# A seven-tile ring for gathered rows, norms made ahead, and the end of an attention laid among mixture blocks

## The chip, the core and the metric

The kernel runs on one core of a Trainium2 chip, as one launch. The core has five engines that work in parallel, each strictly through its own list of instructions: TensorE (PE, matmuls, with the loading of weights shown as PEld), VectorE (DVE), ScalarE (ACT), GpSimd (POOL) and SyncE (SP). They meet only at semaphores. SP and ACT issue plain transfers, POOL issues the indirect ones (a gather or scatter of 128 rows of 128 numbers by a list of row numbers). The metric is the time on the device in microseconds (us), the median of the runs.

## The reference

Two layers over x, 64 sequences of 64 tokens of 128 numbers (4,096 tokens, 32 tiles of 128), in float32:

```
x = x + tanh(g_xattn[0]) * attention0(layernorm(x), ctx, ctx)   # rope, band of 32, 16 heads of 8
x = x + tanh(g_ffn[0])   * mixture0(layernorm(x))               # 64 experts of 88, 8 per token, 1 shared
x = x + tanh(g_xattn[1]) * attention1(layernorm(x), ctx, ctx)   # full in a sequence, biases
x = x + tanh(g_ffn[1])   * mixture1(layernorm(x))               # 8 experts of 512, 2 per token
```

A mixture routes each token to its experts, weighs their results and adds them: `rw` holds 8 (then 2) weights per token, `out[t] = sum_e rw[t,e] * mlp_e(x[t])`.

## The kernel before, in words

Four stages follow each other on PE. **Attention** (L = 0, then 1) is a pipeline over 16 groups of 256 tokens (2 tiles). Step j does six things at once: the front of group j (f), the scores of group j-1 (m), the values of j-2 (v), the output, residual and second norm's statistics of j-3 (b), the router of j-4 (r), and the rank of each row within its expert of j-5 (k). There are 21 steps, so the last five only drain the pipeline.

**The first mixture** (`experts`) takes rows that POOL has scattered by expert into `expert_rows`: 16 shared batches, then 96 routed batches of 4 blocks of 128 rows, 48 for each half of the tokens. Batch by batch, PE turns and multiplies (L729, L747, L762, L775), ACT takes the silu (L985) and copies the result out (L993), DVE multiplies and copies (L1449, L1457), ACT's queue stores 256 KB to `expert_results`. **The combination**: POOL gathers each tile's 8 result rows per token (`gather`, L1634, 8 gathers a tile, 256 in all) and DVE adds them into x with 8 dependent instructions (`combine`, L1539). Tiles 0 to 15 (first half) go into a ring of four tiles in `xn2T`, tiles 16 to 31 into a ring of four in `late_rows`; POOL waits until the tile four before has been combined (`s_comb`). Tiles 0 to 9 are combined during the first mixture, one every four batches and all 8 instructions in a row; the other 22 during attention 1, where `combined_at` names the step.

**Attention 1's first norm** needs x with all 8 results added. DVE takes the statistics of group j at the head of step j (`norm_stats`, L1101, L1105), POOL makes 1/deviation of them (`deviation`, L1660, L1662), DVE the shift `nm` (L1118), ACT applies it (`xn`, L884). POOL's list for step j is: deviation of group j, 6 gathers, the second norm's deviation of group j-3 (same lines), 6 gathers; when the gathers are out, scatters for the second mixture (`scatter_late`, L1641) stand in their place. Before step 0 stand the gathers of tiles 0 to 13.

**The second mixture** (`late_experts`) is 80 blocks of 128 rows: DVE copies weights (L1554), PE multiplies up (L813) and down (L823), ACT takes the gelu (L1022). It begins when attention 1 has drained on every engine. After it POOL gathers the last 32 pieces (L1655), DVE adds them, SP stores x.

**The start**: SP issues the constants, two tables of 576 and 65 KB, 8 tiles of x, nine small inputs behind one count (`S["weights"]`), then the other 24 tiles. PE, ACT (tanh of the gates) and DVE (`split_row`, the bias row in three bf16 parts) all wait for the whole count.

The order is written out by hand: each engine's list is the program text, and no planner moves anything.

## Time and profile before

| | us |
|---|---|
| median of 3 runs (1228.23 to 1237.3) | 1228.86 |
| the profiled execution | 1228.1 |
| its span, first to last instruction | 1226.3 |
| mean granted PE clock, share of full | 0.875 |

The profiled execution is 1.8 us longer than its span and 0.8 us under the median. By the trace, attention 0 runs from the start to about 290 us, the first mixture to 667.1, attention 1 to 1019.8, the second mixture to 1175 and the last gathers, sums and stores to 1226.3. To read it: times of the trace count from the span's start; "idle before <- X" is the time that an engine stood still and the instruction that released it; a transfer is named by its target and source (`expert_results<-arena` is the first mixture's store). Where a step or a batch is spoken of, its start is found in the trace by the instruction that occurs once in each.

### The profile page before, as it was taken

Reading aid. Unit: us, or ns where it says so; the run is one execution under the profiler, and the core shown is the slowest. Engines: PE = TensorE matmul, PEld = TensorE weight load, DVE = VectorE, ACT = ScalarE, POOL = GpSimd, SP = SyncE. Lnnn points to the kernel's source line nnn. Section 1 sums busy time; section 2 is a strip of 40 time slices with the busy share of each in tenths; the row PEclk is TensorE's granted clock in tenths of the full one; section 3 lists DMA queues with packets and bytes.
Section 4 is the critical chain, followed back from the end, with each engine's and each line's share of the span. In section 5 each row is a group of like instructions: output and inputs, shape, how many; then the busy total and the mean of one; then the engine's idle time right before and its main releaser. Section 6 shows DMA issues by size and latency. Waiting matters only on the chain.

```text
span 1226.3 us, 27918 instructions
## 1 busy us (share of the span) xinstructions
PE 968.1 (79%) x8822; PEld 830.1 (68%) x8822; DVE 741.0 (60%) x2638; ACT 600.2 (49%) x1497; POOL 675.9 (55%) x749
## 2 busy tenths in 40 slices
PE   2888889855899999999896357977678778999930
PEld 1666666643699989988896136765556557999930
DVE  3678888866677778655555336567666554334422
ACT  1566666622245545545553143645445535666610
POOL 1106777777777750277555556767767643005445
PEclk9999999966999999999998556668778878999965
DMA  6434666523547765677665222332222112223322
GB/s 184 109 87 118 181 195 175 149 66 103 155 148 216 219 197 161 183 206 207 195 196 161 75 63 75 84 95 77 53 56 83 40 53 69 79 78 109 100 71 66
DMA packets 251184, 151.47 MB, mean 124 GB/s; under 512 B 56179, under 2 KB 236579, under 8 KB 251043
## 3 DMA queue, kind: packets, MB, share of 16 engines
q1 hardware_dynamic: 164706, 68.91, 20.5%
q0 software_dynamic: 20480, 41.98, 11.7%
q10 hardware_dynamic: 65856, 38.81, 10.8%
q8 instruction: 76, 1.25, 0.4%
q14 instruction: 66, 0.53, 0.2%
HBM read 77.24 MB, written 72.35 MB: 122 GB/s over the span
## 4 chain that ended last, share of the span: by engine, by line
PE 51%; DVE 17%; POOL 11%; issue 7%; ACT 6%; DMA 6%; SPq 1%; POOLq 0%; DVEq 0%; ACTq 0%
PE bank L747 6%; PE bank L813 6%; PE bank L823 6%; DVE x L1539 6%; PE bank L775 5%; DMA expert_results<-arena 5%; PE bank L557 4%; PE bank L570 3%; PE bank L762 3%; POOL expert_rows L1619 2%; POOL late_rows L1655 2%; PE bank L729 2%; PE bank L586 2%; PE bank L535 2%; POOL expert_rows L1641 2%
## 5 line engine op out<-in xcount | busy, mean ns | idle before, releaser
L1619 POOL DMA_INDIRECT expert_rows<-xn2T,slot x256 | 250.8, 980 | 88.6 <-issue 82.9
L1634 POOL DMA_INDIRECT xn2T<-expert_results,slot x128 | 122.5, 957 | 131.6 <-DMA expert_results<-arena 61.0
L1634 POOL DMA_INDIRECT late_rows<-expert_results,slot x128 | 123.9, 968 | 48.0 <-issue 36.3
L557 PE MATMUL bank<-cst,work 128*128 128x128 f32 x512 | 96.3, 318 | 51.4 <-ACT sg L943 43.1
L747 PE MATMUL bank<-wexp,arena 128*128 x768 | 135.1, 319 | 0.0
L1655 POOL DMA_INDIRECT late_rows<-expert_results,slot1y x64 | 62.2, 972 | 128.4 <-DMA expert_results<-yb 99.4
L890 ACT ACTIVATE work<-bank 128x512 f32<-128x512 f32 x128 | 76.6, 598 | 96.2 <-PE bank L557 94.4
L775 PE MATMUL bank<-wexp,arena 88*128 x768 | 106.3, 281 | 17.1 <-DVE arena L1457 13.3
L747 PEld LDWEIGHTS bank<-wexp,arena 128*128 128x128 f32 x768 | 114.6, 190 | 5.1 <-issue 1.2
L1022 ACT ACTIVATE arena<-bank,wcopy 128x128 f32<-128x128 f32 x320 | 91.3, 368 | 51.8 <-PE bank L813 51.8
L985 ACT ACTIVATE arena<-bank 128x176 f32<-128x176 f32 x224 | 69.3, 317 | 92.8 <-PE bank L747 52.2
L1457 DVE COPY arena<-bank 88x512 f32<-88x512 f32 x112 | 76.5, 683 | 61.4 <-PE bank L762 57.7
L775 PEld LDWEIGHTS bank<-wexp,arena 88*128 88x128 f32 x768 | 93.1, 191 | 27.4 <-issue 25.4
L557 PEld LDWEIGHTS bank<-cst,work 128*128 128x128 f32 x512 | 64.1, 158 | 61.1 <-issue 57.8
L570 PEld LDWEIGHTS bank<-vm,work 128*64 128x64 f32 x2048 | 81.2, 156 | 32.1 <-ACT work L890 21.3
L993 ACT ACTIVATE arena<-bank 128x512 f32<-128x512 f32 x96 | 57.3, 597 | 87.8 <-DMA expert_results<-arena 50.2
L1449 DVE TENSOR_TENSOR arena<-arena,bank 128x176 f32<-128x176 f32 x224 | 70.7, 333 | 47.2 <-ACT arena L985 45.5
L570 PE MATMUL bank<-vm,work 128*64 128x18 f32 x2048 | 94.3, 227 | 5.0 <-ACT work L890 4.6
L1123 DVE TENSOR_REDUCE nmax<-bank 128x8 fp32r<-128x512 f32 x128 | 85.1, 672 | 9.9 <-PE bank L541 8.5
L884 ACT ACTIVATE xn<-x,nm,rs 128x128 f32<-128x128 f32 x64 | 28.0, 487 | 126.3 <-DVE nm L1118 118.7
L813 PE MATMUL bank<-xgT,wcopy 128*128 128x128 f32 x640 | 86.1, 279 | 1.1 <-DVE wcopy L1554 1.1
L586 PE MATMUL bank<-arena,wqk 128*128 128x256 f32 x192 | 63.6, 445 | 26.6 <-DVE arena L1138 11.4
(207 smaller groups left out, 2118.3 us busy)
## 6 DMA issues: line engine op xcount, KB each, us to landing
arena<-expert_rows SPq DMA_DIRECT2D x384, 64.0 KB
expert_results<-arena ACTq DMA_DIRECT2D x96, 256.0 KB
expert_rows<-zero SPq DMA_DIRECT2D x288, 64.0 KB
arena<-in_ctxT ACTq DMA_DIRECT2D x32, 256.0 KB
expert_rows<-xn2T,slot POOLq DMA_INDIRECT x320
xg<-expert_rows SPq DMA_DIRECT2D x80, 64.0 KB
expert_results<-yb ACTq DMA_DIRECT2D x20, 256.0 KB
wx<-in_mix SPq DMA_DIRECT2D x16, 256.0 KB
```

Source lines behind the costliest of these rows:

```text
L557: mm = pe.transpose(w[:, bb * P:(bb + 1) * P], work[:, u, bb * P:(bb + 1) * P], ident)
L570: mm = pe.matmul(w2[b2 * SEQ:(b2 + 1) * SEQ, at:at + 2 * VW], work2[:, u % 2, pair * P + b2 * SEQ:pair * P + (b2 + 1) * SEQ], vm[:, V % 3, ...
L586: mm = pe.matmul(w[:, h * GTOK:(h + 1) * GTOK], wqk[:, n, h * P:(h + 1) * P], rhs, start=True, stop=True)
L747: mm = pe.matmul(out[:, b * 2 * I0:(b + 1) * 2 * I0], xgT[:, n % 2, 2 * h + b, :], wflat[:, bass.ds(offsets[m][2 * h + b], 2 * I0)], start ...
L775: mm = pe.matmul(bank[7][:, b * P:(b + 1) * P], hT[0:I0, n % 2, b, :], wflat[0:I0, bass.ds(offsets[m][b] + 2 * I0, P)], start=True, stop=T ...
L813: mm = pe.matmul(bank[2 + i % 3][:, c * P:(c + 1) * P], wcopy[:, i % WRING, c * P:(c + 1) * P], xgT1[:, m % 2, i % NB, :], start=True, sto ...
L890: act.activation(work2[:, u % 2, :], (w0, w3, w3, w3)[u][:, :], ACT.Copy).then_inc(S["pt_copied"], 1)
L1022: a = act.activation(hT1[:, i % WRING, c, :], bank[2 + i % 3][:, c * P:(c + 1) * P], ACT.Gelu_apprx_tanh, bias=wcopy[:, i % WRING, F1 + c: ...
L1123: dve.tensor_reduce(nmax[:, u, :], score[u][:].rearrange("p (a k) -> p a k", k=SEQ), AX.X, ALU.max, negate=True).then_inc(S["max_done"], 1)
L1619: pool.indirect_dma_start(xs, bass.IndirectOffsetOnAxis(ap=slot[:, t, k:k + 1], axis=0), xn2all[:, t, :].bitcast(I32), None).then_inc(s_sc ...
L1634: pool.indirect_dma_start(yg[h][:, t // 2 % 2, t % 2, k, :].bitcast(I32), None, ys, bass.IndirectOffsetOnAxis(ap=slot[:, t, k:k + 1], axis ...
L1655: pool.indirect_dma_start(yg1[:, t % 4 * TOPK1 + k, :].bitcast(I32), None, ys1, bass.IndirectOffsetOnAxis(ap=slot1y[:, t, k:k + 1], axis=0 ...
```

## The change

1. **Ring of seven.** Tiles 16 to 31 use a ring of seven tiles: the four of `late_rows` and three in `late_more`, which lies over buffers that the second mixture uses later. POOL waits for the tile seven before. POOL gathers all 16 tiles of the first half before attention 1's steps, then 7, 7, 8 and from step 3 on 10 a step.
2. **Combination.** Eleven tiles instead of ten are combined in the first mixture, two instructions a batch over four batches. `combined_at` is new.
3. **Norms ahead.** The statistics and deviations of attention 1's groups 0 to 4 are made during the first mixture; group g from 5 to 7 in step g-4, from 8 on in step g-1. Their deviations stand between gathers in POOL's list.
4. **Drain among blocks.** Attention 1 ends after 18 steps. What is left of groups 13 to 15 (output, residual, norm, router, ranks) stands as single pieces between the second mixture's blocks 0 to 14, on PE, ACT, DVE and POOL. The second half's block tables move from blocks 2 to 10 to blocks 16 to 24, `place_rows` to 26 to 33. PSUM banks of the second mixture are given out anew (one bank for turned rows, banks 1 and 6 for results).
5. **Inputs by need.** x comes in five parts (2, 6, 8, 8, 8 tiles); constants and the three projections come before the tables; the other small inputs have a count of their own, waited for in step 1 or later, where `split_row` and the tanh now stand.

```diff
-COMBINE_AT = HRTB + 10
-SPACING = 4
-SOONER = (HRTB - 10 + SPACING - 1) // SPACING
+PIECES = 4
+SOONER = 11
+EARLY_GROUPS = SOONER // 2
+LATE_RING = 7
+COMBINE_AT = [HRTB + 7 + t * 11 // 3 for t in range(SOONER)]
+FILL_GATHERS = (7, 7, 8)
-FIRST_GATHERS = 14 * TOPK0
-LATER = 6
+LATER = 5
+PARTS = ((0, 2), (2, 8), (8, 16), (16, 24), (24, 32))
+        def gathered(t):
+            if t < HTILES:
+                return yg[:, t % 4], s_gath[t % 4], (t // 4 + 1) * TOPK0 * 16
+            r, n = (t - HTILES + 4) % LATE_RING, (t - HTILES) // LATE_RING
+            if r < 4:
+                return late_ring[:, r], s_gath[r], (HTILES // 4 + n + 1) * TOPK0 * 16
+            return late_more[:, r - 4], s_more[r - 4], (n + 1) * TOPK0 * 16
+        def late_stats_at(g):
+            return g - 4 if g < HGROUPS else g - 1
...
@@ SP
+            load_x(0)
+            sp.dma_start(cst[:], A["cst"]).then_inc(s_const, 16)
+            first_weights(0, layers[0])
+            sp.dma_start(blk[:], A["sel0"]).then_inc(s_spread, 16)
+            sp.dma_start(blk1[:], A["sel1"]).then_inc(s_spread, 16)
+            load_x(1)
             small(0, layers[0])
-            load_x(1, 4)
+            for part in range(2, len(PARTS)):
+                load_x(part)
...
@@ PE, late_experts
+                pe.wait_ge(S["probs"], GROUPS * 4)
+                pe.wait_ge(S["pt_copied"], GROUPS * 4)
+                pe.wait_ge(S["o_done"], GROUPS * 2)
...
+                    if i == 0: step(FULL, *has_group(FULL), "attn"); step(FULL, *has_group(FULL), "turn")
+                    if i == 1: step(FULL, *has_group(FULL), "out"); step(FULL, *has_group(FULL), "logits")
+                    if i == 4: step(FULL, *has_group(FULL), "rank")
+                    if i == 7: step(FULL + 1, *has_group(FULL + 1), "turn")
+                    if i == 8: step(FULL + 1, *has_group(FULL + 1), "logits")
+                    if i == 9: step(FULL + 1, *has_group(FULL + 1), "rank")
+                    if i == 13: step(FULL + 2, *has_group(FULL + 2), "rank")
...
@@ ACT, late_experts (the exponentials of the router among the gelus)
+                    if i == 3: step(FULL, *has_group(FULL), "exp")
+                    if i == 5: step(FULL, *has_group(FULL), "norm")
+                    if i == 9: step(FULL + 1, *has_group(FULL + 1), "exp")
...
@@ DVE, attention 1
-                        if f: norm_stats(F, F * 2, 2)
+                        if j == 0:
+                            late_neg(EARLY_GROUPS - 1)
+                            combine(SOONER)
+                        if j == 1: split_row()
+                        for g in range(EARLY_GROUPS, GROUPS):
+                            if late_stats_at(g) == j: late_stats(g)
                         if m: max_rows(0)
-                        if f: norm_neg()
...
-                        for t in range(SOONER, TILES):
-                            if combined_at[t] == j: combine(t)
+                        if EARLY_GROUPS <= j + 1 < GROUPS: late_neg(j + 1)
+                        for t in range(SOONER + 1, TILES):
+                            if combined_at(t) == j: combine(t)
...
@@ DVE, experts
-                    if m >= COMBINE_AT and (m - COMBINE_AT) % SPACING == 0:
-                        combine((m - COMBINE_AT) // SPACING)
+                    for t in range(SOONER):
+                        if COMBINE_AT[t] <= m < COMBINE_AT[t] + PIECES:
+                            combine_part(t, m - COMBINE_AT[t])
+                    for g in range(EARLY_GROUPS):
+                        if m == COMBINE_AT[2 * g + 1] + PIECES:
+                            late_stats(g)
+            def combined_at(t):
+                i = t - HTILES
+                return (t - SOONER) // 2 if i < 0 else min(6 + i // 2, max(3, (TOPK0 * (i + 1) - 13) // (2 * LATER) + 4))
...
@@ POOL, attention 1
+            for i in range(HTILES * TOPK0):
                 gather(i)
-            fetched = FIRST_GATHERS
+                g = (i - 4 * TOPK0 - TOPK0 // 2) // (2 * TOPK0)
+                if i % (2 * TOPK0) == TOPK0 // 2 and 0 <= g < EARLY_GROUPS:
+                    late_deviation(g)
+            fetched = HTILES * TOPK0
...
             for j in range(STEPS):
+                fetched, sent = fetch_or_send(j, 2)
+                for g in range(EARLY_GROUPS, GROUPS):
+                    if late_stats_at(g) == j:
+                        late_deviation(g)
+                fetched, sent = fetch_or_send(j, LATER - 2)
+                if 3 <= j < GROUPS + 3:
+                    deviation2(layers[1], j - 3)
+                fetched, sent = fetch_or_send(j, (FILL_GATHERS[j] if j < 3 else 2 * LATER) - LATER)
```

POOL, from the end of the first half's gathers into attention 1's steps 0 to 3. Before (ve and rs are a deviation, of the first or the second norm):

```order
L1634 DMA xn2T<-expert_results,slot 128x128 x12
L1660 TENSOR_SCALAR ve<-mv 128x2
L1662 TENSOR_TENSOR rs<-ve,mhalf 128x2
L1634 DMA xn2T<-expert_results,slot 128x128 x4
L1634 DMA late_rows<-expert_results,slot 128x128 x8
L1660 TENSOR_SCALAR ve<-mv 128x2
L1662 TENSOR_TENSOR rs<-ve,mhalf 128x2
L1634 DMA late_rows<-expert_results,slot 128x128 x12
```

Now, the same place (27 gathers are what follows group 4's deviation, the third pair of ve and rs is the second norm of group 0):

```order
L1762 DMA xn2T<-expert_results,slot 128x128 x27
L1762 DMA late_more<-expert_results,slot 128x128 x9
L1788 TENSOR_SCALAR ve<-mv 128x2
L1790 TENSOR_TENSOR rs<-ve,mhalf 128x2
L1762 DMA late_more<-expert_results,slot 128x128 x7
L1788 TENSOR_SCALAR ve<-mv 128x2
L1790 TENSOR_TENSOR rs<-ve,mhalf 128x2
L1762 DMA late_more<-expert_results,slot 128x128 x8
L1788 TENSOR_SCALAR ve<-mv 128x2
L1790 TENSOR_TENSOR rs<-ve,mhalf 128x2
L1762 DMA late_rows<-expert_results,slot 128x128 x3
```

The first deviation that a step waits for no longer stands behind the gathers of its own step.

DVE, from the end of one full step of attention 1 into the next (the two L1539/L1654 rows are the combination; `nmax` is the first instruction that PE's scores wait for). Before:

```order
L1287 SCALAR_TENSOR_TENSOR wk<-wk,gates,wsum 128x4
L1539 SCALAR_TENSOR_TENSOR x<-late_rows,wk,x 128x128 x8
L1101 BN_STATS st<-x 128x6 x2
L1105 BN_AGGR mv<-st 128x2 x2
L1123 TENSOR_REDUCE nmax<-bank 128x8
L1118 SCALAR_TENSOR_TENSOR nm<-mv,rs 128x2
```

Now, between steps 4 and 5, with one tile:

```order
L1350 SCALAR_TENSOR_TENSOR wk<-wk,gates,wsum 128x4
L1639 SCALAR_TENSOR_TENSOR nm<-mv,rs 128x2
L1654 SCALAR_TENSOR_TENSOR x<-late_more,wk,x 128x128 x8
L1183 TENSOR_REDUCE nmax<-bank 128x8
L1262 TENSOR_REDUCE top<-sg 128x2
```

The shift `nm` of the next group is made before the combination, and the step begins with no wait for a norm.

ACT, at the second mixture's first blocks (L1022 and L1085 are the gelus, x4 for a block). Before:

```order
L1015 ACTIVATE xgT<-bank 128x512
L1022 ACT_TABLE_LOAD
L1022 ACTIVATE arena<-bank,wcopy 128x128 x8
L1015 ACTIVATE xgT<-bank 128x512
L1022 ACTIVATE arena<-bank,wcopy 128x128 x16
```

Now:

```order
L1085 ACTIVATE arena<-bank,wcopy 128x128 x4
L950 ACTIVATE aT<-bank 128x256
L986 ACTIVATE ysb<-bank 128x256
L1085 ACTIVATE arena<-bank,wcopy 128x128 x4
L995 ACTIVATE sg<-bank 128x16
L1078 ACTIVATE xgT<-bank 128x512
L1085 ACTIVATE arena<-bank,wcopy 128x128 x8
L999 ACT_TABLE_LOAD
L999 ACTIVATE sc<-choice 128x16
L1085 ACT_TABLE_LOAD
```

The router's exponentials of groups 14 and 15 (L999) now stand among the gelus, each with a table load before it and one behind it: four loads more.

## Rows read from the trace of the kernel before

**Rows 1.** The page: engines, and PE's granted clock in 40 slices of the span

```profile
PE 968.1 (79%) x8822; PEld 830.1 (68%) x8822; DVE 741.0 (60%) x2638; ACT 600.2 (49%) x1497; POOL 675.9 (55%) x749
PEclk9999999966999999999998556668778878999965
```

**Rows 2.** Waits in 668 to 1020 us: engine, line <- releaser: us, times, longest

```profile
ACT xn L884 <- DVE nm L1118: 118.7, 16, 21.2
PE bank L557 <- ACT sg L943: 43.1, 11, 6.1
DVE nm L1118 <- POOL rs L1662: 37.2, 16, 12.0
```

**Rows 3.** Windows: length, busy us (instructions) of each engine, clock, DMA share, GB/s

```profile
118.14:132.55 14.41, 12.79 (x163) 9.78 (x160) 12.41 (x61) 9.55 (x22) 10.62 (x12) 1.00 0.52 138
804.52:822.97 18.45, 16.41 (x131) 12.99 (x131) 11.40 (x46) 9.86 (x23) 13.60 (x17) 0.54 0.22 58
842.46:859.72 17.26, 12.75 (x147) 10.37 (x147) 11.49 (x46) 9.53 (x23) 13.51 (x17) 0.82 0.22 58
859.72:879.49 19.77, 12.48 (x147) 9.96 (x147) 13.88 (x53) 9.66 (x23) 13.50 (x16) 0.91 0.22 58
1003.00:1019.80 16.80, 7.18 (x44) 5.05 (x42) 9.37 (x52) 3.70 (x12) 10.78 (x12) 0.50 0.11 36
1019.80:1175.00 155.20, 154.53 (x1365) 153.73 (x1365) 58.84 (x207) 101.29 (x340) 37.99 (x38) 0.99 0.31 89
```

**Rows 4.** Timeline of POOL in attention 1: start, us, instruction [idle before <-releaser]

```profile
665.46 0.94 POOL L1634 DMA_INDIRECT xn2T<-expert_results,slot  x1 [3.69 <-DVE x L1539]
686.79 1.06 POOL L1634 DMA_INDIRECT xn2T<-expert_results,slot  x1 [10.57 <-DVE x L1539]
754.07 0.72 POOL L1662 TENSOR_TENSOR rs<-ve,mhalf 128x2 f32<-128x2 f32 x1
...
857.16 0.94 POOL L1634 DMA_INDIRECT late_rows<-expert_results,slot  x1 [0.31 <-issue]
858.41 0.94 POOL L1634 DMA_INDIRECT late_rows<-expert_results,slot  x1 [0.30 <-issue]
859.39 0.24 POOL L1660 TENSOR_SCALAR ve<-mv 128x2 f32<-128x2 f32 x1
860.63 1.06 POOL L1634 DMA_INDIRECT late_rows<-expert_results,slot  x1 [0.19 <-issue]
...
943.51 0.72 POOL L1662 TENSOR_TENSOR rs<-ve,mhalf 128x2 f32<-128x2 f32 x1
```

**Rows 5.** Waits in 539 to 668 us, the first mixture with combinations

```profile
PE bank L775 <- DVE arena L1457: 11.6, 10, 3.0
```

**Rows 6.** Timeline of the first mixture: a combination, a batch without, the last matmuls

```profile
566.93 3.08 DVE L1539 SCALAR_TENSOR_TENSOR x<-xn2T,wk,x 128x128 f32<-128x128 f32 x8
575.35 0.69 DVE L1457 COPY arena<-bank 88x512 f32<-88x512 f32 x1 [1.08 <-PE bank L762]
...
665.93 1.15 PE L775 MATMUL bank<-wexp,arena 88*128 x8 [3.02 <-DVE arena L1457]
```

**Rows 7.** Timeline of the first 30 us

```profile
12.95 2.05 PE L607 MATMUL bank<-wv,arena 128*128 128x128 f32 x8 [12.95 <-DMA brow<-in_L_ffn_gate_bias]
15.90 1.64 DVE L1101 BATCH_NORM_STATS2 st<-x 128x6 f32<-128x128 f32 x8
24.84 0.76 DVE L1138 TENSOR_TENSOR arena<-bank,cst 128x256 f32<-128x256 f32 x2 [2.01 <-PE bank L586]
```

**Rows 8.** DMA: issues of the whole program, KB each, median us to landing

```profile
x<-in_x SPq DMA_DIRECT2D x4, 512.0 KB, 7.9
```

**Rows 9.** Timeline of ACT at attention 1's first scores

```profile
703.73 0.84 ACT L875 ACTIVATE vm<-bank,cst 128x256 f32<-128x256 f32 x2
704.59 1.28 ACT L894 ACT_TABLE_LOAD   x1
705.88 0.60 ACT L894 ACTIVATE work<-bank 128x512 f32<-128x512 f32 x1
```

More of the change, by code:

```diff
@@ L841, in _ @@
             experts()
-            attention(1)
-            late_experts()
+            late_experts(attention(1))
         @block.scalar
```

331 lines of the change are left out of this document (202 added, 129 removed).

## The prediction

> **What bounds the kernel now.** I read the page first: PE is busy for 79% of the span, and its granted clock is at full speed everywhere but in attention 1 (0.5 to 0.9 there) [rows 1]. So attention 1 is where the kernel is not limited by matmuls. The waits of that stretch say by what: ACT stands 118.7 us before `xn`, for the shift `nm`, 16 times, PE stands 43.1 us at the head of its steps behind ACT, and DVE itself waits 37.2 us for POOL's deviation [rows 2]. The windows give the step: 17.26 us with one tile combined, 19.77 with two, with PE busy for under 12.8 [rows 3]. POOL's timeline names the limit of the 17.26: twelve gathers with a pitch of 1.25 us (857.16, 858.41) and two deviations of about 1.1 us each (859.39 to the next gather's normal place) make 12 x 1.25 + 2 x 1.1 = 17.2 [rows 4]. And it shows a backlog: POOL stood 3.69 and 10.57 us for tiles not yet combined, with tiles 13 to 31 still to fetch [rows 4]. In the first mixture PE waits 11.6 us, 10 times, for DVE's copy behind a combination [rows 5]. The second mixture is PE alone, 154.5 of 155.2 us, and before it lie 16.8 us of draining with PE busy for 7.2 [rows 3].
>
> **The change, part by part.** All times are against the profiled execution's span of 1226.3 us.
>
> *Start.* First matmuls began at 12.95, when the last of nine small inputs had landed, DVE took 8 tiles of statistics at 15.90, after the bias row, and its first rotation began at 24.84 [rows 7]. Now two tiles of x and the projections come first, but DVE's list has the statistics of parts 0, 1 and 2 ahead of that rotation. Part 2 is issued at about 8 us (some 16 issues of 0.5); the four x loads took 7.9 us in the median [rows 8], so it lands at 12 to 16. Statistics (8 tiles, 1.64) and their sums (0.64) follow: rotation at about 16.4, 8.4 us sooner. The bias row, 2.7 us of DVE, now stands in step 1, where DVE's rotations are waited for. Term: **-6** (bounds 0 and -9).
>
> *First mixture.* A combination of 3.08 us stands in front of a copy that otherwise comes after an idle 1.08 us [rows 6]. Two instructions cost 3.08/4 = 0.77 and fit in that gap; where two tiles overlap (four batches) 1.55 stand there, and five batches have statistics of 0.73 besides, about 0.5 us over the gap, which PE's other matmuls cover (a combination 2 us over the gap cost PE only about 1). The 11.6 us go, 3.0 of them at the very end. Term: **-11** (bounds -4, if the 256 KB stores, which compete with gathers here, become the next limit, and -13).
>
> *POOL's backlog.* What ends step 3 is the second norm's first deviation, at 754.07 [rows 4]. I count what stands before it. Tile 13's gathers end near the mixture's end (667.1 by [rows 6], less 11: 656), tile 14 starts at about 657.5, since POOL still stands for group 4's statistics at batch 92. Up to the deviation come 16 + 22 + 5 gathers and four deviations: 43 x 1.25 + 4 x 1.1 = 58.2, so 716, 38 us sooner, 11 of which are counted. With a ring of seven no gather waits for a combination there. Steps 0 to 2 of PE need no POOL (their norms exist) and are done by about 700, so POOL decides. Term: **-28** (bounds -20 and -33).
>
> *Steps 4 to 13.* Before: 943.51 - 754.07 = 189.4 us [rows 4]. Now POOL's floor is 10 x 1.25 + 1.1 = 13.6 a step, 14.7 with a first-norm deviation. PE's own step is 17.26 less the 3.5 us that it stood at its head, 13.8. A step with one tile then takes about 14.5. With two tiles DVE reaches the next scores' maximum 3.1 us later, which nothing covers: 17.2; four of these ten steps follow such a pair (steps 5, 9, 11, 12). With 3 us for a start at the low clock: 4 x 17.2 + 6 x 14.5 + 3 = 159. Attention 0 shows that PE, DVE and ACT can hold such a step: 14.41 us with more work on each [rows 3]. Term: **-30** (bounds -42, POOL's floor alone, and 0).
>
> *From there to the first block.* Before, 943.5 to 1019.8: 76.3 us. Now, after the deviation of step 13: 3.5 to its end, 17.2, 14, then 10 us into step 16 the 25th scatter is out; seven more (8.8) complete the first half, about 3 us to land and be seen, 2 to load rows, 1.2 to turn and copy them: 60 to 61. PE's own steps 16 and 17 end about when the scatters do. Term: **-15** (bounds -22 and -3).
>
> *Second mixture.* The pieces bring PE about 5 us: three ranks, two turns, two routers, one output, at the durations they have in a step. Four table loads of 1.28 us, in pairs of 2.8 with the exponential, delay ACT, whose lead covers half of it: 3.5. Term: **+8.5** (bounds +3, and +25 if the whole drain of 16.8 us comes back too). The load's row shows 1.28 us and the next activation 0.01 later, the one before ended just ahead of it [rows 9]. The Trainium skill (ScalarE: Activation LUTs, What ACT_TABLE_LOAD costs) puts a switch at 1.283 us and 1.38 of drain, 2.66 in all, and advises to group functions by table, which speaks against this placing. By that price the term would be about 5 us larger; the row has no such drain.
>
> The tail of 51 us does not change: 32 gathers after the last store. Sum: -6 - 11 - 28 - 30 - 15 + 8.5 = -81.5. Span 1144.8, execution 1.8 more, 1146.6; the profiled execution was 0.8 under the median: **1147**.
>
> **The rivals.**
>
> *PE stays at the low clock in attention 1.* There the step was 18.45 us with PE busy for 16.41 at a clock of 0.54 [rows 3], so steps 4 to 15 would take 12 x 18.45 = 221 us where I count 159 + 17.2 + 14 = 190: +31, 1178. For it: the clock came back and fell again every few steps. Against: it fell after steps with a hole of several us at their head, and these holes go; attention 0 with small holes keeps 1.00. The Trainium skill (TensorE: Matmul & The Clock Gate, A second HAM failure mode: psum-queue depth-cycling) tells of a kernel in which short idles between groups of matmuls were enough to make the clock swing; attention 0's rows speak against that here.
>
> *Two-tile steps cost nothing.* DVE has slack elsewhere in the step, and POOL's floor alone counts: -12, and the stores stay hidden: 1133.
>
> *The drain's waits come along.* The drain took 16.8 us with PE busy for 7.2 [rows 3]. If PE, at the head of a block, stands for each piece as it did there, those 16.8 us go into the blocks: 1164. Against: a block gives each answer 1.9 us of other work to come in (155.2 us for 80 blocks). POOL's deviation of group 15, behind five scatters, is the worst of them.
>
> *Slower: a circle between POOL and DVE.* DVE stands at the end of a step for a tile whose gathers POOL has queued behind the deviation of that same step's second norm, which waits for DVE. Each step would then be POOL's 14.7 in a row with DVE's 10 us up to the residual: 24.7 instead of about 16, over 13 steps +113: 1260. It decides from the point where a tile's last gather stands behind the deviation of the step that combines it; by the schedule all but tile 31 are out by the step before, so it needs POOL to fall a whole step behind. Break-even would be a step of about 22 us.
>
> *The norm's wait hides another.* The change does what it says, but behind `nm` stands a chain of the same length (scores, maximum, shift, exponential, turn), so that steps 4 to 13 stay at 18.9 us and only the other terms are won: 1177. For it: ACT's and PE's waits at the head overlap, and one hides the other in the trace. Against: attention 0 has the same chain, with more in it, at 14.41 [rows 3].
>
> **Chances.** Forecast 52%; low clock 15%; cheap two-tile steps 11%; waits in the drain 8%; steps of the old length 6%; circle 4%; the rest, something between these and the old time, 4%. The likeliest case's range by its bounds is 1130 to 1165. With the low clock and the drain's waits the range is **1120 to 1187**. All but the circle and part of the rest are more than 1% (12 us, about what a measurement of this kernel can tell) under 1228.9: faster 0.91, same 0.04, slower 0.05.
>
> **What would show it.** ACT's wait for `nm` of 118.7 us should be under 15; PE's clock in attention 1 at 0.9 or more after step 5; the first second-norm deviation of attention 1 near 710 (716 less the start's 6), the 11th near 869; first rotation near 16; the first block of the second mixture near 930; the stretch of the 80 blocks about 164 us. I am wrong if POOL stands for `s_comb` in attention 1, if the step with one tile is over 16 us, or if PE stands for pieces in the blocks by more than 10 us in sum.

## The result and the profile after

| | us |
|---|---|
| before, median of 4 runs | 1228.6 (1225.5 to 1237.3) |
| changed, median of 4 runs | 1165.1 (1161.5 to 1175.2) |
| ratio | 0.948, 95% interval 0.943 to 0.953 |
| changed, profiled execution | 1161.9, span 1160.1 |

The change took 5.2% off the time, inside the range and 18 us above the predicted 1147. The spans, 1226.3 and 1160.1, are compared by stage below. Each stage ends at a row of the trace: the sixth scores of attention 0; the first and the last matmuls of "down" (an expert's second multiplication) in the routed batches of the first mixture; the first and the eleventh `rs` of a second norm in attention 1; the first and the last matmuls of the second mixture's blocks. Lengths in us:

```
stage                                  before   after  moved  forecast
start, to the sixth scores (date)        95.1    92.9   -2.2     -6
first mixture                           314.8   304.6  -10.2    -11
from there to the first rs, attn 1       87.3    65.3  -22.0    -28
steps 4 to 13 (first to eleventh rs)    189.4   157.4  -32.0    -30
from there to the first block            76.3    69.6   -6.7    -15
80 blocks                               154.3   160.5   +6.2     +8.5
tail                                     52.2    52.5   +0.3      0
```

The start is a date, and the 257 us between it and the mixture are not in the table; 0.4 us of the start's gain were gone by the mixture. With that the moves make 66.2. Lengths here and below are taken from dates rounded to 0.1 us.

One of the later kernels (`six_rows`) had a run more than 1.5% above its fastest, which its ratio leaves out.

The page of the changed kernel, for [rows 1]:

```profile
PE 959.5 (83%) x8822; PEld 820.9 (71%) x8822; DVE 735.3 (63%) x2639; ACT 603.5 (52%) x1501; POOL 678.6 (58%) x751
PEclk9999999985999999999999868959877769999965
```

The work is the same, the idle time is shorter, and the clock still dips in attention 1 (slices 23 to 33). The waits of attention 1, 656 to 947 us (columns as in [rows 2]):

```profile
DVE nm L1232 <- POOL rs L1790: 35.4, 15, 13.1
PE bank L579 <- DVE nmax L1183: 22.3, 11, 4.6
PE bank L590 <- DVE arena L1210: 15.5, 6, 10.9
ACT xn L936 <- DVE nm L1639: 0.4, 1, 0.4
```

ACT's 118.7 us before `xn` are 0.4, and PE no longer stands for `sg`. The longest that is left is one wait of 13.1 us for POOL in step 3 (PE's 10.9 is its shadow); DVE's other 14 waits for `rs` make 22.3 us, and PE stands for the maximum, up to 4.6 us. Windows of the changed kernel (columns as in [rows 3]): 5 us at the end of step 5 and the 5 behind them, two steps at the full clock, three that were not, and the 80 blocks:

```profile
745.00:750.00 5.00, 2.78 (x29) 2.03 (x28) 2.12 (x12) 3.42 (x8) 4.08 (x6) 0.85 0.24 57
750.00:755.00 5.00, 5.00 (x47) 3.60 (x46) 4.34 (x17) 1.82 (x5) 3.78 (x5) 0.50 0.27 87
785.85:799.30 13.45, 11.19 (x147) 8.71 (x147) 10.56 (x44) 9.63 (x24) 10.71 (x14) 1.00 0.28 70
832.00:845.04 13.04, 11.11 (x147) 8.75 (x148) 10.92 (x46) 9.67 (x24) 10.29 (x14) 1.00 0.23 63
750.72:769.78 19.06, 19.06 (x149) 15.19 (x148) 14.05 (x53) 10.00 (x24) 12.91 (x16) 0.50 0.27 72
845.04:865.58 20.54, 16.23 (x148) 12.75 (x148) 15.19 (x61) 10.19 (x24) 14.60 (x18) 0.64 0.24 63
881.58:902.87 21.29, 16.67 (x152) 13.44 (x152) 15.13 (x61) 10.08 (x24) 10.25 (x13) 0.66 0.12 38
947.10:1107.60 160.50, 159.17 (x1397) 158.02 (x1397) 65.01 (x246) 108.53 (x353) 58.62 (x61) 0.98 0.34 96
```

The same 147 to 149 matmuls take 13.0 us at 1.00 and 19.1 at 0.50, where PE is busy all the time. POOL at the mixture's end and at the two ends of steps 4 to 13, for [rows 4]:

```profile
647.80 0.22 POOL L1788 TENSOR_SCALAR ve<-mv 128x2 f32<-128x2 f32 x1 [4.73 <-DVE mv L1632]
...
662.90 0.94 POOL L1762 DMA_INDIRECT xn2T<-expert_results,slot  x1 [0.30 <-issue]
...
720.14 0.72 POOL L1790 TENSOR_TENSOR rs<-ve,mhalf 128x2 f32<-128x2 f32 x1
...
877.49 0.72 POOL L1790 TENSOR_TENSOR rs<-ve,mhalf 128x2 f32<-128x2 f32 x1
```

Tile 14's first gather is the row at 662.90, the twelfth behind group 4's deviation. Between the mixture and the first `rs`, POOL stands for a combination for 0.3 us in all. Before, it stood for 22.3, in three waits: the 10.57 us of [rows 4] and

```profile
715.54 0.94 POOL L1634 DMA_INDIRECT late_rows<-expert_results,slot  x1 [7.81 <-DVE x L1539]
...
740.32 0.94 POOL L1634 DMA_INDIRECT late_rows<-expert_results,slot  x1 [3.91 <-DVE x L1539]
```

The first mixture, 539 to 655 us, for [rows 5]; ACT's wait there was 18.0 us, 14 times, before:

```profile
ACT arena L1056 <- DMA expert_results<-arena: 47.0, 35, 2.3
PE bank L818 <- ACT arena L1056: 1.5, 4, 0.7
PE bank L818 <- DVE arena L1540: 0.9, 1, 0.9
```

PE's waits for DVE's copy (11.6 us before) are down to 0.9; ACT waits for the stores instead. The first rotations, for [rows 7], as DVE had them:

```profile
15.32 1.65 DVE L1163 BATCH_NORM_STATS2 st<-x 128x6 f32<-128x128 f32 x8 [1.55 <-DMA x<-in_x]
17.56 0.72 DVE L1198 TENSOR_TENSOR arena<-bank,cst 128x256 f32<-128x256 f32 x2
```

### The profile page after: what moved, and what is told of

The parts are those of the page before. It is cut to its first block, busy times and chain, and to the rows that moved or that the text cites. A ratio compares the mean times of both kernels' runs of the same rounds, so it can differ in the third digit from the quotient of the medians.

```text
span 1160.1 us, 28026 instructions
## 1 busy us (share of the span) xinstructions
PE 959.5 (83%) x8822; PEld 820.9 (71%) x8822; DVE 735.3 (63%) x2639; ACT 603.5 (52%) x1501; POOL 678.6 (58%) x751
## 3 DMA queue, kind: packets, MB, share of 16 engines
q0 software_dynamic: 20480, 41.98, 12.6%
q10 hardware_dynamic: 65856, 38.81, 11.3%
q8 instruction: 76, 1.25, 0.5%
## 4 chain that ended last, share of the span: by engine, by line
PE 51%; POOL 16%; DVE 13%; issue 8%; DMA 7%; ACT 3%; SPq 1%; DVEq 0%; POOLq 0%; ACTq 0%
PE bank L790 7%; PE bank L818 6%; PE bank L860 6%; PE bank L870 6%; DMA expert_results<-arena 6%; PE bank L805 3%; POOL late_rows L1762 3%; PE bank L772 3%; POOL late_more L1762 3%; PE bank L603 3%; PE bank L590 3%; POOL expert_rows L1743 3%; POOL late_rows L1783 2%; DVE x L1654 2%; PE bank L568 2%
## 5 line engine op out<-in xcount | busy, mean ns | idle before, releaser
L942 ACT ACTIVATE work<-bank 128x512 f32<-128x512 f32 x128 | 76.6, 599 | 91.8 <-PE bank L590 90.0
L1085 ACT ACTIVATE arena<-bank,wcopy 128x128 f32<-128x128 f32 x320 | 91.1, 371 | 48.0 <-PE bank L860 48.0
L590 PE MATMUL bank<-cst,work 128*128 128x128 f32 x512 | 94.7, 314 | 23.4 <-DVE arena L1210 15.5
L603 PEld LDWEIGHTS bank<-vm,work 128*64 128x64 f32 x2048 | 78.6, 152 | 29.7 <-ACT work L942 19.4
L603 PE MATMUL bank<-vm,work 128*64 128x18 f32 x2048 | 91.5, 224 | 4.5 <-ACT work L942 4.1
L1183 DVE TENSOR_REDUCE nmax<-bank 128x8 fp32r<-128x512 f32 x128 | 85.0, 673 | 14.3 <-PE bank L574 10.7
L946 ACT ACTIVATE work<-bank 128x512 f32<-128x512 f32 x128 | 76.2, 595 | 32.6 <-PE bank L579 32.1
L579 PE MATMUL bank<-nmax,idr 128*128 128x512 f32 x128 | 67.1, 525 | 25.9 <-DVE nmax L1183 25.9
L619 PE MATMUL bank<-arena,wqk 128*128 128x256 f32 x192 | 63.1, 441 | 29.9 <-DVE arena L1198 16.4
L590 PEld LDWEIGHTS bank<-cst,work 128*128 128x128 f32 x512 | 62.3, 156 | 33.4 <-issue 29.9
```

Of the source, the lines that this page charges most:

```text
L590: mm = pe.transpose(w[:, bb * P:(bb + 1) * P], work[:, u, bb * P:(bb + 1) * P], ident)
L603: mm = pe.matmul(w2[b2 * SEQ:(b2 + 1) * SEQ, at:at + 2 * VW], work2[:, u % 2, pair * P + b2 * SEQ:pair * P + (b2 + 1) * SEQ], vm[:, V % 3, ...
L942: act.activation(work2[:, u % 2, :], (w0, w3, w3, w3)[u][:, :], ACT.Copy).then_inc(S["pt_copied"], 1)
L1085: a = act.activation(hT1[:, i % WRING, c, :], bank[2 + i % 3][:, c * P:(c + 1) * P], ACT.Gelu_apprx_tanh, bias=wcopy[:, i % WRING, F1 + c: ...
L1183: dve.tensor_reduce(nmax[:, u, :], score[u][:].rearrange("p (a k) -> p a k", k=SEQ), AX.X, ALU.max, negate=True).then_inc(S["max_done"], 1)
```

## The experiments

Each kernel is the changed one with the edit shown. A ratio is to runs of the kernel before on the same chip, whose medians lay between 1224.7 and 1236.6 us, so kernels are compared by their ratios and intervals, and stages by the profiles. Stages as above; the start is in the first column as the date of the sixth scores. One profiled execution each.

```
kernel              start mixture  to rs  steps   way  blocks    span
changed              92.9   304.6   65.3  157.4  69.6   160.5  1160.1
norms_in_step        92.4   306.1   73.2  184.9  68.6   159.6  1194.6
drain_first          94.1   305.2   65.1  157.3  88.8   155.6  1175.7
old_order            94.7   304.2   64.5  158.9  69.6   160.4  1160.6
whole_combination    94.3   315.9   61.4  163.7  69.6   160.4  1175.4
six_rows             93.0   304.4   57.6  156.0  69.5   160.2  1150.2
half_combination     94.0   304.1   65.1  151.7  59.9   159.2  1141.5
ring4                93.9   304.7   65.4  163.9  65.0   159.7  1162.1
filled_hole          93.0   303.6   65.5  157.8  64.9   159.7  1154.3
spread_combination   94.1   305.0   65.5  156.5  64.8   159.7  1155.5
filled_holes         92.7   305.0   65.4  163.3  64.2   160.0  1160.5
store_now            94.7   297.9   65.3  160.6  65.2   159.3  1152.9
three_together       92.7   297.8   65.5  151.4  63.5   159.7  1140.5
```

How far to trust a row: old_order, store_now and drain_first do the same work in steps 4 to 13 as the changed kernel and took 157.3 to 160.6 us; on the way to the first block, store_now and ring4 took 65 where the changed kernel took 69.6, with nothing edited there. So in attention 1 a difference under 4 or 5 us between two profiles says nothing. Nor is a profiled execution always near its kernel's median: those of filled_holes (1162.3 us, the other three 1148.6 to 1153.7) and spread_combination (1157.3, the others 1147.5 to 1151.4) were the slowest of their four. Ratios of different chips need the same care: on the chip of filled_holes, spread_combination and store_now the kernel before ran from 1224.8 to 1238.5 us, with a median of 1236.6.

**Norms in their own step.**

```diff
-                        for g in range(EARLY_GROUPS, GROUPS):
-                            if late_stats_at(g) == j: late_stats(g)
+                        if f: late_stats(F)
                         if m: max_rows(0)
+                        if f: late_neg(F)
...
+                if j < GROUPS:
+                    late_deviation(j)
```

(and no statistics or deviations in the mixture; POOL makes each deviation at the head of its step)

> The changed kernel (profiled 1161.9 us) with one part undone: the statistics and deviations of second attention's first norms stand at the head of their own steps again, on DVE and POOL; ring, drain and input order stay. My theory: the wait for the shift nm held each step's head, so ACT stands some 100 us before xn again, the stretch from the first second-norm deviation to the eleventh grows from 157 us to about 185, and the first such deviation comes about 5 us later, with five deviations of 1.1 us more in steps 0 to 4. In all about 1161.9 + 28 + 5 = 1195 us. Rival: the ring alone freed POOL, whose floor of 14.7 us a step decides either way; then the kernel stays within 6 us of 1162, and the same chain of maximum, shift and exponential takes the place of the wait.

Measured: 1198.5 us, ratio to before 0.976 (0.974 to 0.978); steps 4 to 13 grew by 27.5, the stretch ahead of them by 7.9. Its waits, 670 to 960 us:

```profile
ACT xn L936 <- DVE nm L1632: 107.3, 16, 18.1
```

The wait for `nm` set the step. This one part carries about half of the whole gain. The added time ahead of the steps is waiting of another kind: POOL stood 16.9 us for statistics there, and for no combination.

**The drain ahead of the blocks.**

```diff
-                slots(step, FULL if L else STEPS)
+                slots(step, STEPS)
...
                     if piece:
+                        return
```

> The changed kernel with one part undone: second attention runs its last three steps to the end before the first block of the second mixture; nothing of them stands among the blocks. My theory: the drain of before comes back, 16.8 us with PE busy for 7.2, less the 4 us or so by which the first rows wait for POOL's scatters in any case; the 80 blocks go back from 161 us to 155. Net about +5 to +9 us, 1169. Rival A: the scatters alone decide when the first block can start (it starts at 947.1, the last of the first half's 32 scatters was issued at 937.4), so the drain hides behind them and the kernel gains the 6 us of the blocks: 1156. Rival B: the table loads cost more than the rows tell, so that the blocks shrink by over 8 us.

Measured: 1177.8 us, 0.959 (0.954 to 0.963). The way to the first block is 19.2 us longer, the blocks 4.9 shorter: +14.3, more than I expected, since PE waits again for `xn2T`:

```profile
945.69 0.69 PE L668 MATMUL bank<-cst,xn2T 128*128 128x128 f32 x2 [1.48 <-ACT xn2T L978]
959.47 0.69 PE L668 MATMUL bank<-cst,xn2T 128*128 128x128 f32 x2 [8.44 <-ACT xn2T L978]
965.13 0.17 PE L686 MATMUL bank<-total,ones 128*1 128x8 bf16 x1 [3.32 <-DVE slot L1386]
```

The 8.44 us are POOL's: its last deviations stand behind ten scatters each, 943.81 and 957.59 in its timeline. Rival A (scatters decide) is out; so is B, since the pieces with their four table loads cost the blocks 4.9 us.

**The old order of inputs.**

```diff
+            sp.dma_start(cst[:], A["cst"]).then_inc(s_const, 16)
+            sp.dma_start(blk[:], A["sel0"]).then_inc(s_spread, 16)
+            sp.dma_start(blk1[:], A["sel1"]).then_inc(s_spread, 16)
             load_x(0)
...
             small(0, layers[0])
+            first_weights(0, layers[0])
```

> The changed kernel with one part undone: the constants and both tables of the spread go out ahead of x, and the three projections after the other small inputs, as in the kernel before; the statistics stay in five parts. The changed kernel's first scores came 7.3 us sooner than before, but from the sixth step on only 2.15 us of it were left. My theory: steps 1 to 5 are set by DVE's work for setup (statistics of 8 tiles each, the bias row), not by the first step's date, so undoing the order costs about 2 us: first scores near 27, sixth step within 3 us of 93, kernel about 1164. Rival, as I had forecast: a start sooner by 6 us moves everything behind it, and the kernel comes to 1168.

Measured: 1162.7 us, 0.948 (0.944 to 0.951), the changed kernel's ratio. Its sixth scores came at 94.7, within the 92.4 to 94.7 of the kernels that keep the new order. By these dates the order of the inputs is worth no more than 2 us.

**Combination in one piece.**

```diff
-                        if COMBINE_AT[t] <= m < COMBINE_AT[t] + PIECES:
-                            combine_part(t, m - COMBINE_AT[t])
+                        if m == COMBINE_AT[t] + PIECES - 1:
+                            combine(t)
```

> The changed kernel with one part undone: in the first mixture each tile's combination is again one piece of eight instructions (3.08 us), at the batch in which its last pair of instructions stood; number of tiles, statistics and POOL's order stay. My theory: PE's waits for DVE's copy come back, about 1.2 us for each of 11 tiles, and the routed batches from the first combination on go from 3.20 us to about 3.43: +10 us, 1172. Rival: in the changed kernel ACT already stands 83 us for the stores of 256 KB, which hide part of such a wait; then PE loses less than 5 us and the kernel stays under 1167.

Measured: 1181.2 us, 0.962 (0.960 to 0.964); the mixture is 315.9 us, before's 314.8. Between 539 and 668 us PE stood again:

```profile
PE bank L818 <- DVE arena L1540: 15.1, 11, 3.2
```

So the pieces are all of the mixture's gain. With this the parts undone one by one account for the whole change: as ratios the norms are worth 0.028, the drain 0.011 and the pieces 0.014, together 0.053, against 0.052 that was won; each of the ratios has an interval of 0.002 to 0.005 to either side. (The rest of the +16 lies in steps 4 to 13, at the edge of what a profile tells.)

**Six rows fetched in place of eight.** `gather` returns for the second half where k > 5; the combination reads row k % 6, so two of the eight results are left out and two are counted twice.

```diff
+                if h and k > 5:
+                    return
```

> The changed kernel, in which POOL fetches only six of the eight rows of each token of the second half (the combination uses two of them twice, so the result is not the reference's): 32 gathers of 1.25 us, 40 us of POOL's work, are gone from second attention; PE's, DVE's and ACT's work is the same. My theory: POOL's total bounds second attention (its backlog makes DVE stand 13.1 us and PE 10.9 in step 3, and its floor of 14.7 us stands in every step), so the first second-norm deviation comes 7 to 8.75 us sooner and steps 4 to 13 go from 157.0 us to 140 to 145: 1162 - 22 = 1140. Rival: DVE's two-tile steps and TensorE's low clock set the steps by themselves; then only the 8 us of the backlog are won: 1154.

Measured: 1148.2 us, 0.933 (0.925 to 0.941). The rival was right: 7.7 us ahead of the first rs, 1.4 in the steps. POOL had time to spare there and stood for DVE (710 to 880 us), while PE still stood for the maximum:

```profile
POOL ve L1790 <- DVE mv L1225: 23.4, 8, 5.8
POOL ve L1790 <- DVE mv L1632: 20.0, 7, 5.6
PE bank L579 <- DVE nmax L1183: 14.6, 6, 3.9
```

**Half of each combination.** Tiles 12 to 31 get four of their eight results.

```diff
+                    if t > SOONER and k % 2:
+                        continue
```

> The changed kernel, in which DVE does only four of the eight instructions of each combination in second attention (tiles 12 to 31; the result is not the reference's): 20 x 4 x 0.38 = 30 us less of DVE's work; POOL's gathers, PE and ACT are the same. My theory in the prediction: a second tile in a step delays the next maximum by 3.1 us, and PE stands for it (PE stands 12.2 us for the maximum between 720 and 877, twice about 4.5), so steps 4 to 13 go from 157.0 us to about 149, and about 4 us more are won up to the first block: 1150. Rival: POOL's floor is behind all of it (16 steps of 14.7 us), DVE's relief moves only who waits, and the kernel stays within 3 us of 1162.

Measured: 1141.6 us, 0.930 (0.925 to 0.936): 5.7 us in the steps and 9.7 on the way to the first block, of which some 5 also came in kernels without an edit there. DVE's combinations count, POOL's gathers alone do not.

**A ring of four.**

```diff
-LATE_RING = 7
+LATE_RING = 4
```

> The changed kernel with a ring of four tiles in place of seven for the second half's gathered rows; the three other tiles' space stays unused, all steps and combinations stand where they stood. With seven no gather of tiles 16 to 22 waits for a combination of its own half; with four, tile 20 waits for tile 16's (step 3), 21 for 17's (step 4), and so on. My theory: POOL stands several us in each of steps 4 to 12, the deviations queued behind those gathers come later, and DVE waits for them in its own step: steps 4 to 13 grow by 15 to 40 us, kernel 1180 to 1200. Rival: POOL stands little, because its gathers are late anyway (its timeline shows it standing for DVE 13.6 us in those steps), and the kernel stays within 6 us of 1162; then the second half's tiles could have done with four, and the gain in the backlog came from the norms alone.

Measured: 1166.7 us, 0.952 (0.946 to 0.958); in profile 2 us over the changed kernel, 6.5 more in the steps and 4.6 less behind them. My theory missed: the steps grew by 6.5 where I had 15 to 40, though POOL did stand for combinations behind 722 us, 14.4 us in five waits. The first rs came at the same distance (65.4), with 0.6 us of such waits ahead of it: no gather there needs the longer ring.

**The hole of step 3 filled.**

```diff
                         pe.wait_ge(S["k_read"], F + 1)
+                        if L == 1 and F == 3:
+                            for again in range(26):
+                                pe.matmul(w0[:, 0:GTOK], wqk[:, 0, 0:P], xnT[:, F % 2, :], start=True, stop=True)
```

> The changed kernel with 26 more matmuls of PE in step 3 of second attention, each the same projection of q into the same bank as the one behind them (the result is the same), in the place where PE stands for 10.9 us until POOL's first second-norm deviation is through. TensorE's granted clock was at 0.50 in 659 to 687, 715 to 723 and 747 to 779 us; the two steps in the last of these took 19.1 and 16.1 us, against 13.4 to 14.3 of the two ahead and of the one behind. My theory: the hole takes the clock down later; without it steps 6 and 7 take about 14.5 us each and the eleventh second-norm deviation comes some 5 us sooner: 1157. Rival: what takes the clock down is how the ordinary steps fill PE (small idles of 0.5 to 1 us), or POOL's floor takes the place of the clock; then the stretch is unchanged within 2 us.

Measured: 1159.8 us, 0.946 (0.941 to 0.952). The stretch that was at 0.52 in the changed kernel, and the next one (columns as above):

```profile
747.00:779.00 32.00, 25.29 (x317) 19.92 (x317) 25.12 (x100) 21.63 (x51) 24.21 (x30) 0.95 0.43 111
793.00:823.00 30.00, 29.09 (x226) 23.43 (x227) 22.10 (x88) 15.80 (x38) 20.44 (x24) 0.50 0.20 56
```

PE had been busy for 96% of the stretch at 0.52 and was busy for 79% of it at 0.95; but the low stretch had moved, not gone. The steps took 157.8 us, as the rival said.

**More holes filled.** The edit above with 22 projections of q, 3 more in each of steps 5 and 9, and more projections of v in steps 6, 9, 10, 12, 13 and 14.

```diff
+                        for again in range({6: 6, 9: 4, 10: 14, 12: 26, 13: 12, 14: 28}.get(F, 0) if L else 0):
+                            pe.matmul(w1[:, 0:P], ctxT[:, F % 2, 0, :, :], wv[:], start=True, stop=True)
```

> The changed kernel with PE's holes in second attention filled: more matmuls, each the same as one that follows it into the same bank (results the same), 22 in step 3, 3 each in steps 5 and 9 (projection of q, 0.44 us each at the low clock), and 6, 4, 14, 26, 12, 28 of the projection of v (0.14 us each at the full clock) in steps 6, 9, 10, 12, 13, 14, where PE stands 1 to 4.6 us for the maximum or the queries. With the hole of step 3 alone filled the low stretch 747 to 779 was gone, but another one came at 793 to 823. My theory: TensorE's clock is what makes these steps long (at 1.00 a step takes 13.0 to 14.3 us, at 0.50 to 0.66 it takes 16 to 21); with the holes filled its mean between 720 and 877 goes from 0.80 to above 0.92, steps 4 to 13 to about 148 us, where POOL's floor stands, the kernel to about 1147. Rival: the clock falls all the same by holes that were not filled, or the extra matmuls take what the clock gives; then the kernel comes to 1155 to 1165.

Measured: 1152.5 us, 0.933 (0.927 to 0.938), below the changed kernel's interval, but the profiled execution, the slowest of the four, was the changed kernel's, 1160.5. Its mean clock over steps 4 to 13 was 0.86, short of the 0.92 that I had wanted. Two parts of it can be compared with the changed kernel, from the scores of one step to those of another:

```
                     filled_holes            changed
steps 4 to 7     69.5 us, clock 0.71    62.8 us, clock 0.74
steps 8 to 13    94.8 us, clock 0.98    95.7 us, clock 0.86
```

The 5.9 us that the steps took longer were lost in steps 4 to 7, where the clock had fallen. In steps 8 to 13 it was up, and they were no shorter for it: PE did more work in them, and between 720 and 880 us ACT stood 23.2 us for the late v (9.4 in the changed kernel). So in this execution my theory in its plain form fell: a full clock bought with matmuls in the steps' path did not shorten them. What made the three other executions 9 to 14 us faster, at mean clocks of 0.914 to 0.923 against 0.908, no profile shows.

**The combination in the step's middle.**

```diff
                         if m: max_rows(3)
+                        due = [t for t in range(SOONER + 1, TILES) if combined_at(t) == j]
+                        for t in due[:1]: combine_part(t, 0); combine_part(t, 1)
                         if b: norm2_neg()
                         if r: choose(0); count_late_rows()
                         if f: bias_queries()
+                        for t in due[:1]: combine_part(t, 2); combine_part(t, 3)
...
-                            if combined_at(t) == j: combine(t)
+                        for t in due[1:]: combine(t)
```

> The changed kernel with one thing moved: in second attention the first tile due in a step is combined in its middle, four of the eight instructions (1.55 us) in front of the wait for POOL's second-norm deviation, where DVE stands about 2 us in an ordinary step (2.09 at 797.5), four behind the biased queries; only a second tile stays at the step's end. Work, gathers and result are the same. My theory, from the kernel with half the combinations (steps 4 to 13 5.3 us shorter, and 10 us more up to the first block, with all of POOL's work in place): the combinations at the step's end are what lets PE stand for the maximum and takes the clock down; moved, steps 4 to 13 come to about 151 us, the way to the first block to 62 to 66, the kernel to about 1150. Rival: DVE's 30 us less were what counted, not their place; then the kernel stays within 3 us of 1162, or loses up to 5 us because outs and queries come later.

Measured: 1150.2 us, 0.931 (0.926 to 0.937). In profile the steps took 156.5 us, no less than the changed kernel's: the clock lay at 0.50 from 720 to 750. Behind that, four steps followed at a pitch of 14.7 to 14.8 us, POOL's floor (770.0 to 829.1). The profiled execution was again the slowest of four, so what this edit is worth in the steps is left open.

**Stores at once.**

```diff
-                    if n >= SHB: keep_rows(n - SHB)
-                    if n > SHB: store_rows(n - SHB - 1)
-                store_rows(RTB - 1)
+                    if n >= SHB: keep_rows(n - SHB); store_rows(n - SHB)
```

> The changed kernel with one thing moved: in the first mixture ACT issues each batch's store of 256 KB right behind the copy that fills it, not behind the copy of the next batch, so that each store has one batch (3.1 us) more before its buffer is wanted. ACT stands 83.4 us for stores in the changed kernel, 64 times. My theory: nearly all of this wait goes, and with it what PE loses by it, which is little: PE is busy for 111.5 of 113 us between 512 and 625, and stands 3.3 us for ACT's copies in all. So the mixture's 304.6 us shrink by 2 to 4 us, the kernel to 1158 to 1160. Rival A, the lower bound of my prediction: the stores are the next limit, and the batches with combinations go from 3.2 us to 3.06: 6 us or more. Rival B: ACT now stands for its own copy before each issue, or gathers and loads get slower; no gain or up to 3 us lost.

Measured: 1155.3 us, 0.934 (0.927 to 0.940); the mixture is 6.7 us shorter, rival A. ACT no longer waits for a store; it waits for PE instead. From the first combination on nearly all batches run at 3.05 to 3.2 us, where every third or fourth of the changed kernel took 3.3 to 3.95. One such batch of the changed kernel:

```profile
573.27 1.45 PE L790 MATMUL bank<-wexp,arena 128*128 x8
574.55 0.60 PE L772 MATMUL bank<-cst,arena 128*128 128x128 f32 x4
575.48 1.15 PE L818 MATMUL bank<-wexp,arena 88*128 x8 [0.33 <-ACT arena L1056]
576.47 0.60 PE L805 MATMUL bank<-cst,arena 128*88 128x128 f32 x4
```

The row names 0.33 us; from the batch's start to the next (576.91) it is 3.64, 0.6 over the others. I had taken the sum of such waits (3.3 us) for the price.

**Three edits together:** stores at once, the middle of the step, and 22 projections in the hole of step 3.

> The changed kernel with three edits together: each store of the first mixture issued right behind its copy (alone it took 6.7 us from the mixture), the first tile of a step combined in the step's middle (alone 5.1 us from the way between the eleventh second-norm deviation and the first block, and steps of 14.7 to 14.8 us where the clock stayed up), and PE's hole of step 3 filled with 22 more projections (alone the low stretch 747 to 779 was gone). If the three parts are independent: the mixture ends 6.7 us sooner, the first second-norm deviation comes at about 714, steps 4 to 13 run at POOL's pace of 14.75 us and take 148 us, 62 to 65 us follow to the first block (926), and the kernel comes to 1139 to 1143. Rival: the low clock comes back elsewhere between 790 and 880, as it did behind the filled hole alone, and steps 4 to 13 stay at 156: then 1147 to 1150.

Measured, in 6 runs: 1142.0 us, 0.928 (0.923 to 0.933), below the changed kernel's interval (0.943 to 0.953): a version that beats both. The profile shows 6.8 us won in the mixture, 6.0 in the steps and 6.1 behind them; its median is 8 and 13 us below those of the middle of the step and of the stores alone, measured on another chip, but the intervals of the ratios overlap. Filling the hole shows no part in it, though no kernel has the other two edits without it: the clock was at 0.50 from 720 to 740 us all the same, and the third second-norm `rs`, at 747.44, came 18.7 us behind the one ahead. From the fifth second-norm `rs` to the eleventh POOL's timeline shows nothing but its floor, 14.75 us a step:

```profile
776.32 0.72 POOL L1792 TENSOR_TENSOR rs<-ve,mhalf 128x2 f32<-128x2 f32 x1
...
791.11 0.72 POOL L1792 TENSOR_TENSOR rs<-ve,mhalf 128x2 f32<-128x2 f32 x1
...
805.81 0.72 POOL L1792 TENSOR_TENSOR rs<-ve,mhalf 128x2 f32<-128x2 f32 x1
...
864.82 0.74 POOL L1792 TENSOR_TENSOR rs<-ve,mhalf 128x2 f32<-128x2 f32 x1
```

## Why the prediction was right, and where it was not

*Start, -6 forecast, -2.2 got.* The first rotation came at 17.56 (16.4 forecast), the first scores 7.3 us sooner. The step that failed is the one from there on: I took off 2.7 us for the bias row and let the rest carry through. But steps 1 and 2 took 13.2 and 14.2 us where before they took 11.3 and 12.6, steps 4 and 5 another 1.5 us more than before, and by the sixth scores 2.2 us were left. With the old order the kernel took the same time, so the term is nil to 2 us. The bias row stands between the two rotations of step 1; which of DVE's pieces takes the rest was not tried.

*First mixture, -11 forecast, -10.2 got.* Shown by undoing it (+11.3). The lower bound that I had named, stores of 256 KB as the next limit, was half true: they held another 6.7 us, which issuing them sooner gave.

*POOL's backlog, -28 forecast, -22.0 got.* The date that failed is tile 14's start: I put it at 657.5, and it was 662.90. POOL stood 4.73 us for group 4's statistics and had 11 gathers to do behind them. From 662.90 my count of 43 gathers and four deviations holds: 58.2 us, to 721, and that `rs` ended at 720.9. My sum was 0.6 us off besides: 38.4 us sooner less the 11 of the mixture is 27.4, not 28.

My reason was wrong in a part. What went is POOL's standing for combinations between the mixture and the first `rs`: 22.3 us before, 0.3 now, which is the 22.0 that was won, since POOL's list in between is about as long (50 gathers, now 49). I had put this down to the ring of seven; the ring of four has 0.6 us of it and gives the same stretch. So it was the sooner combinations or the shorter steps 0 to 2 (from the scores of step 1 to those of step 2 and on to those of step 3 it is 14.7 and 14.1 us, 29.4 and 25.0 before) that freed POOL; no kernel separates the two. With the norms undone POOL does not stand for combinations either, but for statistics, and 7.9 us come back.

*Steps 4 to 13, -30 forecast, -32.0 got.* Shown: the norms undone bring 27.5 of them back. But the make-up of the new step was partly luck. I had 14.5 us for a step behind one tile and 17.2 behind two; the rows have 13.0 to 13.5 where the clock is full and 16 to 21 where it is not. A sign of being wrong that I had named, a step with one tile over 16 us, came up too: step 7, behind one tile and mostly at the low clock, took 16.1 us from its scores to the next. The clock was 0.80 between 720 and 877, so my sign "0.9 or more after step 5" was wrong: the rival of the low clock came true for part of the steps. In profile neither fewer gathers (-1.4) nor the filled hole (+0.4) nor more matmuls for the clock (+5.9) shortened them alone; less combining gave 5.7, and three edits together 6.0, of which the last six steps stand at POOL's floor. The last two are just outside what a pair of profiles can tell.

*From there to the first block, -15 forecast, -6.7 got.* I had priced steps 14 and 15 at 17.2 and 14 us; they fell into a low clock (0.66 and 0.71) and, the first, into a wait of 4.6 us for the maximum, and took 21.3 and 16.3. Other kernels with the same work there took 65, so 4 of the missing 8 us are a matter of where the low clock falls.

*Blocks, +8.5 forecast, +6.2 got.* PE stood 2.3 us in them, the pieces cost 4.9 by the undone drain. The load's row says 1.28 us again, with the exponential 0.01 us behind it:

```profile
957.89 1.28 ACT L999 ACT_TABLE_LOAD   x1
959.18 0.22 ACT L999 ACTIVATE sc<-choice 128x16 f32<-128x16 f32 x1
959.42 1.28 ACT L1085 ACT_TABLE_LOAD   x1
```

What the Trainium skill adds (ScalarE: Activation LUTs, What ACT_TABLE_LOAD costs), a drain of 1.38 us, is not in these rows. The Trainium skill's advice to batch activations by table set (ScalarE: Activation LUTs, Table sets: the hidden batching unit) speaks against this placing; here the four extra loads are part of the 4.9 us that the pieces cost the blocks, and placing the drain there saved 14.3 us net of them.

The signs held where they concern waits (`xn` 0.4 us, no POOL standing for `s_comb` in attention 1, PE's 2.3 us in the blocks), and the dates of attention 1 came 8 to 17 us late: 720 and 877 for 710 and 869, and the first block at 947 for 930.

## What to carry to other kernels

When a wait at the head of a pipelined step goes, look at once for what stood ready behind it: here an in-order engine's bulk work at the step's end, and a queue's floor (ten gathers of 1.25 us and two deviations of 1.1), which after three edits was all that was left in the last six of these steps. Cut such bulk work into pieces that fit the gaps in which the engine stands anyway. A wait row tells who released whom, not what the wait costs: price it by the pitch of the repeating unit with and without it, as the batches of 3.06 and 3.64 us did.

## What the runs showed of the hardware

- PE's granted clock goes down in attention 1 behind stretches in which PE is partly idle: 2.78 of 5 us busy, then 30 us at 0.50. In that low stretch PE is busy for 97% of the time (29.9 of 30.7 us from 748.5), so its busy share hides the loss. It is not so in every one: from 850.9 to 868.0 PE is busy for 14.5 of 17.1 us at 0.50, from 656.4 to 687.1 for 16.6 of 30.7. The 10.9 us hole moved the next low stretch, it did not decide whether there was one (747 to 779, or 793 to 823 with the hole filled). The two-level clock (1.2 and 2.4 GHz by its shares of 0.50 and 1.00) makes a step of 13.0 us one of 19.1. I had held attention 0's rows against the Trainium skill (TensorE: Matmul & The Clock Gate, A second HAM failure mode: psum-queue depth-cycling), which tells of a clock that swings when PE idles briefly between groups; here, in attention 1, the rows side with the skill: from 745 to 750, ahead of a fall, PE's longest idle before one row was 1.4 us.
- Issuing each store one batch sooner took away the 83 us that ACT stood for stores, and 6.7 us of the mixture, though PE's own rows named 3.3 us of waiting and had it 98% busy.
